# Pre-norm Fourier-attention and gated-MLP layer: wider weight transfers, a fold by column halves, smaller constants, and a new order on five engines

## What is computed

```python
xn = layernorm(x)
q, kv = heads(xn @ W_q.T), heads(xn @ W_kv.T)
qf, kvf = fft(q), fft(kv)                       # along the 32 of a head
qf, kvf = qf / norm(qf), kvf / norm(kvf)        # complex l2 norm of each head
kvf = cumsum(kvf, axis=sequence)
x = x + real(ifft(qf * kvf)) @ W_o.T
h = layernorm(x)
gate = silu((h @ fp8(gate_w)) * gate_scale)
up = (h @ fp8(up_w)) * up_scale
x = x + ((gate * up) @ fp8(down_w)) * down_scale
```

## Time and profile before

| | us |
|---|---|
| time, median of 3 runs | 422.43 (421.98 to 422.79) |
| the profiled execution, its own time | 422.47 |
| its span, first to last instruction | 420.7 |
| TensorE busy | 411.4 (98%) |
| VectorE busy | 281.6 (67%) |
| ScalarE busy | 193.4 (46%) |
| GpSimd busy | 101.9 (24%) |

### The profile page before, as it was taken

The page is one execution under the profiler, slowest core; times in us unless marked ns, Lnnn a source line. Parts: engine busy times, 40 slices in busy tenths (PEclk is TensorE's granted clock), DMA queues, the critical chain, the costliest instruction groups (busy, mean ns, idle before and its releaser), DMA issues.

```text
span 420.7 us, 5465 instructions
## 1 busy us (share of the span) xinstructions
PE 411.4 (98%) x1895; PEld 219.1 (52%) x1895; DVE 281.6 (67%) x496; ACT 193.4 (46%) x322; POOL 101.9 (24%) x107
## 2 busy tenths in 40 slices
PE   8999999899999999999999999999999999999994
PEld 4744454355555554454554564454555555555553
DVE  5998998989999695187685953176774744322234
ACT  3687656576746245436322573255342522132220
POOL 0133641014244222045450031043441001300002
PEclk9999999999999999999999999999999999999999
DMA  8996547600281153241112025320122041200002
GB/s 261 266 247 238 171 106 182 145 2 0 60 240 28 28 74 76 50 151 49 27 27 51 0 50 89 63 81 20 25 27 51 0 89 30 82 2 0 2 0 100
DMA packets 57546, 33.54 MB, mean 80 GB/s; under 512 B 49456, under 2 KB 49840, under 8 KB 57392
## 3 DMA queue, kind: packets, MB, share of 16 engines
q1 hardware_dynamic: 57232, 33.19, 30.9%
q10 hardware_dynamic: 288, 0.02, 0.0%
HBM read 17.44 MB, written 4.19 MB: 51 GB/s over the span
## 4 chain that ended last, share of the span: by engine, by line
PE 79%; SPq 3%; DVE 3%; issue 1%; DMA 1%; POOL 0%; ACT 0%; DVEq 0%
PE bd L447 21%; PE bg L431 20%; PE bu L431 20%; PE ba L348 10%; PE ba L388 7%; SPq L1583 2%; PE ba L361 1%; DMA hT<-ks 1%; SPq L1609 1%; DVE xn L1019 0%; DVE bst L1104 0%; DVE h L1101 0%; DVE zT L1076 0%; SPq L1570 0%; DVE gu L988 0%
## 5 line engine op out<-in xcount | busy, mean ns | idle before, releaser
L447 PE MATMUL bd<-dw,fu 128*128 128x512 f32 x376 | 100.2, 411 | 0.0
L431 PE MATMUL bg<-hT,gu 128*128 128x512 f16 x384 | 91.0, 380 | 1.3 <-DMA hT<-ks 1.3
L431 PE MATMUL bu<-hT,gu 128*128 128x512 f16 x384 | 90.7, 379 | 0.0
L447 PEld LDWEIGHTS bd<-dw,fu 128*128 128x128 f32 x376 | 70.6, 188 | 18.6 <-DVE fu L1146 0.7
L1141 DVE SCALAR_TENSOR_TENSOR ff<-bu,us,sl 128x512 f32<-128x512 f32 x48 | 35.9, 748 | 66.1 <-PE bu L431 62.9
L697 ACT ACTIVATE sl<-bg,gs 128x512 f32<-128x512 f32 x48 | 33.0, 687 | 81.1 <-PE bg L431 80.1
L348 PE MATMUL ba<-wf,xT 128*128 128x512 f16 x288 | 63.2, 379 | 0.0
L431 PEld LDWEIGHTS bu<-hT,gu 128*128 128x128 f16 x384 | 37.6, 98 | 45.3
L431 PEld LDWEIGHTS bg<-hT,gu 128*128 128x128 f16 x384 | 34.9, 98 | 47.8 <-issue 10.2
L1146 DVE TENSOR_TENSOR fu<-ff,fu 128x512 fp32r<-128x512 f32 x47 | 40.0, 852 | 15.7 <-ACT fu L703 15.3
L1504 POOL TENSOR_TENSOR h<-ff,h 128x512 f32<-128x512 f32 x14 | 17.6, 1276 | 129.9 <-DVE ff L1163 129.9
(11 more groups left out here) (174 smaller groups left out, 447.9 us busy)
## 6 DMA issues: line engine op xcount, KB each, us to landing
h<-x_dram SPq DMA_DIRECT2D x16, 256.0 KB, 4.2
out_dram<-h SPq DMA_DIRECT2D x16, 256.0 KB, 2.0
hT<-w_q_dram SPq DMA_DIRECT2D x4, 256.0 KB, 3.7
gu<-w_kv_dram SPq DMA_DIRECT2D x4, 256.0 KB, 4.0
hT<-gate_w_dram SPq DMA_DIRECT2D x2, 512.0 KB, 4.0
hT<-up_w_dram SPq DMA_DIRECT2D x2, 512.0 KB, 6.2
gu<-woT_dram SPq DMA_DIRECT2D x1, 1024.0 KB, 5.2
hT<-down_w_dram SPq DMA_DIRECT2D x2, 512.0 KB, 5.0
```

What stands on the lines that cost most here:

```text
L431: m = e.matmul(bk[:, :], gu[:, c, 4 * w + k, col:col + P], hT[:, b % 2, part, k, :], start=k == 0 and part == 0, stop=k == KT - 1 and part ...
L447: m = e.matmul(bd[t][:, :], fu_at(n)[:, part, P * t:P * t + P], dw[:, i, :], start=i == 0 and part == 0, stop=i == NI - 1 and part == 1)
```

## The change

- W_q and W_kv come in four transfers of two blocks (512 KB) and not in eight of one block; the host lays them out by pairs of blocks. `sum_w` waits for its pair.
- The constant for `pe_heads` is no longer part of `cst`; GpSimd writes it (five memsets, `pool_heads`) into a tile of its own, and `cst` is 128 columns. `dve_head` now waits for `cst`, `pe_heads` for the memsets.
- A bank of the fold holds two slices k and the 256 columns of two blocks, where it held one slice k and all 512 columns. So the first two banks are complete after blocks 0 and 1; `act_wf` and `dve_wf` run on such banks, and `pe_qk` waits for both column halves of a pair of slices.
- `EPS` is a bias in ScalarE's root (from the tile `eps`, a GpSimd memset), and `root0_head` on VectorE is gone. `dve_xl` is gone: `pool_xl` does all tiles.
- One warm-up matmul fewer; `act_first_root` and `dve_one` stand later.
- All five engines have a new order, in the opening, in block 0 and in the loop.

The diff, cut to its core (of the orders, a few lines):

```diff
-        cst = sb("cst", [P, 384], F32)
+        cst = sb("cst", [P, 256], F32)
+        heads = sb("heads", [P, P], F32)
...
+    def folds(w):
+        return [piece for g in range(2) for piece in (("heads", w, g), ("fold", w, g, 0), ("fold", w, g, 1))]
...
         def pe_fold(e, w, f):
-            j = KT * w + f
+            j, g = KT * w + f, f // 2
...
-                if f == 0:
-                    vacant(e, ("fold", w, k))
-                m = e.matmul(ba[AT["fold", w, k]][:, P * f:P * f + P], raw[w][:, f, P * k:P * k + P], fs[:, j, :],
+                if f % 2 == 0 and k % 2 == 0:
+                    vacant(e, ("fold", w, g, k // 2))
+                at = 256 * (k % 2) + P * (f % 2)
+                m = e.matmul(ba[AT["fold", w, g, k // 2]][:, at:at + P], raw[w][:, f, P * k:P * k + P], fs[:, j, :],
...
-                        e.wait_ge(v_wf, 4 * w + k + 1)
+                        e.wait_ge(v_wf, 4 * w + 2 + k // 2 + 1)
...
         def act_root0(e, b, ts):
-            piece = roots_of(b, ts[0])
-            e.wait_ge(v_r1, 2 * piece + 1)
-            e.activation(E1[:, 1, ts[0]:ts[-1] + 1], E1[:, 0, ts[0]:ts[-1] + 1], ACT.Sqrt).then_inc(a_rt0, 1)
+            g = slice(ts[0], ts[-1] + 1)
+            e.wait_ge(p_eps, 1)
+            e.wait_ge(v_mv1, 2 * (4 * b + ts[-1]) + 2)
+            if b > 0:
+                e.wait_ge(v_r1, roots_of(b, 0))
+            e.activation(E1[:, 0, g], mv1[:, g, 1], ACT.Sqrt, bias=eps[:, :]).then_inc(a_rt0, 1)
...
-        def dve_xl(e):
-            e.wait_ge(a_xh, 1)
-            e.tensor_tensor(xs[:, 0, 1, :], xn[:, 0, :], xs[:, 0, 0, :], ALU.subtract).then_inc(v_xl, 1)
...
+        def pool_heads(e):
+            e.memset(heads[:, :], 0.0).then_inc(p_heads, 1)
+            e.wait_ge(p_heads, 1)
+            for q in range(0, P, HD):
+                e.memset(heads[q:q + HD, q:q + HD], 2.0 ** -14).then_inc(p_heads, 1)
...
-        def sp_raw(e, w, f):
-            e.dma_start(raw[w][:, f, :], (w_q, w_kv)[w][P * f:P * f + P, :]).then_inc(d_raw[w][f], 16)
+        def sp_raw(e, w, g):
+            src = (w_q, w_kv)[w][P * g:P * g + P, :]
+            e.dma_start(raw[w][:, 2 * g:2 * g + 2, :], src.rearrange("p (f n) -> p f n", f=2)).then_inc(d_raw[w][g], 16)
```

715 lines of the change are left out of this document (354 added, 361 removed).

## The result

The changed kernel is slower. Median of 5 runs: 426.49 us (425.13 to 427.21), against 422.43 us (421.42 to 422.79) for the kernel before; the ratio is 1.0084, 95% interval 1.0062 to 1.0107. The prediction was 421.1 us with a range up to 423.7. The profiled execution took 426.49 us, its span 424.7 at a granted clock of 0.998.

A forecast was written before the change was run, and what follows sets the result against it. TensorE was taken as the bound, busy 332.55 of 332.70 us, so only its waits could be won. 422.47 - 0.1 (stretch to 45 us) - 1.3 (hT) = 421.1 us, range 419.6 to 423.7.

The forecast's parts named there:

- W_o's state: TensorE's start of the work behind the last high part of W_o: 45.07 us before, forecast at 44.95.
- The opening, steps 1 to 5: Walk to TensorE's second projection: reached at 19.2 us instead of 20.06, 0.8 earlier, range 0.3 to 1.6.
- Step 4: Opening: the transposed input tile 0 lands at 13.6 to 14.4 us, up to 15.4 with full rings.
- step 5: Opening: VectorE's last remainder of folded W_q at about 16.1 us; projection ends at 17.4, two folds make it 19.2.
- Steps 1 to 3: Opening: second pair of W_q at 7.9 us, W_q folded at 12.3, first two folds of W_kv until about 14.3.
- The point on the table load: Opening, ScalarE: a load of 1.28 us between first sum and root, 5.7 to 6.9, is hidden.
- Tile 3: Projection of input tile 3: transposes land at 32.9 us, TensorE arrives at 32.4, a new wait of 0.5 (0 to 1.5).
- W_o: Preparation of W_o: TensorE waits 1.1 us for ScalarE's copy; 0.1 us of the opening's gain is left.
- The wait for hT: Before the first gate matmul: SyncE starts hT's transfers at 66 us, so the whole 1.3 us wait goes.
- The rival "the wait for hT stays": SyncE's queue: the first hT transfer begins at 69 again, the eight take 10 us, time 422.2 us; chance 0.18.
- The rival on VectorE: MLP of block 0: VectorE is late for the first `dve_f`, or the same in the loop, 423.7 us; chance 0.18.
- The rival "opening not shorter": Opening: transposed tile 0 lands at 16 or later, everything to 45 us about 0.8 late, 422.0 to 423; chance 0.11.

The follow-up runs named there:

- the run with the old attention: Changed kernel with block 0's attention, from the second projection to the last dve_hT, in the order of the kernel before: 424.20 us, ratio 1.0037.
- the run with the opening alone: Changed opening, then every engine's remaining work and the loop in the order of the kernel before: 422.53 us, ratio 1.0008 to the kernel before.
- the old loop: Changed kernel with the loop over b = 1 to 3 in the order of the kernel before on all five engines: 426.28 us, ratio 1.0104.

## Why the prediction was wrong, point by point

*What bounds the kernel*: right. TensorE has the same work at the same clock, and the time is what it waits. Against the forecast of 421.1 the changed kernel is 5.4 us longer. W_o's state came 1.9 us later than forecast (46.89, not 44.95), another 2.0 were lost from there to the first gate matmul (84.73, not 80.75: the 1.41 us for hT, and 0.56 us for the transposed z at 57.27, of which the forecast has nothing), and 1.5 behind it, where the forecast took none. No single term explains the direction; the steps that failed follow.

*The opening, steps 1 to 5*: 19.2 forecast, 20.96 in this profile, outside the range of 0.3 to 1.6 us early. Step 4 held: the transposed tile 0 landed at 14.1. In step 5 the last remainder ended at 17.7 and not at 16.1, but the projection, begun at 16.59, did not wait for it. Steps 1 to 3 failed. In this profile the first pair of W_q came late (VectorE's sum at 5.98, 4.54 before), but that is not the reason: in the fourteen other profiles with the same opening that sum begins at 4.69 to 5.53, and TensorE's second projection is still never earlier than 20.00 and up to 21.83. What they share is the order. VectorE's first scalings of `fs` now stand behind the statistics of the second input tile, and wait for its transfer; the clearest case is the run with the old attention:

```profile
7.38 0.69 DVE L1012 BATCH_NORM_STATS2 bst<-h 128x6 f32<-128x512 f32 x1 [1.93 <-DMA h<-x_dram]
...
8.72 0.71 PE L343 MATMUL ba<-fs,hT 128*128 128x128 f32 x4 [1.73 <-DVE fs L984]
```

From the first fold on, all fifteen take 12.7 to 13.7 us to the second projection (12.8 here), where the kernel before takes 12.55 (7.51 to 20.06): the reordering shortens nothing there. Two waits stand in each of them that steps 2 and 3 put at nothing: 0.36 to 0.42 us for the sums of W_kv, ahead of the last fold of W_q (12.47 here), and 0.40 to 0.45 us for the scalings of `fs` beside GpSimd's low part (14.35 here). The move of the low part was counted as 0.6 us taken off VectorE, and it gave 0.9 and 0.5 us back on the two pairs of scalings beside it. The point on the table load held, the load was hidden behind the wait for the second pair:

```profile
6.72 1.28 ACT L620 ACT_TABLE_LOAD   x1
8.02 0.48 ACT L620 ACTIVATE E<-mv,eps 128x1 f32<-128x1 f32 x2
8.40 0.61 ACT L612 ACTIVATE tu<-hT 128x512 f32<-128x512 f32 x1
```

The load begins 0.02 us after the sum's last row has ended (6.70), and the activation behind it starts 0.02 us after its end. The Trainium skill, "ScalarE: Activation LUTs", What ACT_TABLE_LOAD costs, puts a drain of some 1380 ns on top; the trace does not show it here either. And the opening as a whole had the smaller say: the run with the opening alone was 0.5 us late at 20 us and not at all at the end.

*Tile 3*: a wait of 0.5 was forecast and 0.64 came, by luck. The landing time was about right (2.6 to 3.3 us), but ScalarE's high part came at 30.65 and not at 28.1, held by the sums over W_o and a half that waited for their transfers, and TensorE was 2.3 us later than forecast as well (34.67, not 32.4), so that the difference stayed. For tile 2 no wait was forecast, and 0.32 came: the step left out that its transposes stand in a queue into which the same diff puts W_o 5 us earlier, where they took 6.0 to 7.7 us. With the high part of tile 3 early, its transposes met that queue too and took 5.0 to 5.2.

*W_o*: the wait before its fourth part was forecast at 1.1 us and TensorE's state at 44.95. The wait was 0.20 and the state 46.89. The premise "counted from VectorE's clock" was right, but VectorE's clock was not 0 to 1.1 us earlier, it was later: it scaled kv tiles 2 and 3 at 44.16 (42.33). I had set the statistics moved ahead against the work removed and called it even; this is the step that failed. VectorE's first norm alone, behind three more statistics and the late projections, was 3.0 us later than before (33.23, 30.27), and the scaling 1.8.

*The wait for hT*: forecast gone, measured 1.4. Two rows say why:

```profile
70.02 12.26 SPq L1593 DMA_TRANSPOSE hT<-ks  x8
...
77.42 0.69 DVE L1131 TENSOR_TENSOR ks<-qk,ks 128x512 f16<-128x512 f32 x1 [0.53 <-ACT ks L699]
```

The step that failed is the start of SyncE's transfers: 70.02 and not 66. The transposes of an input tile at 65.70, which wait 1.3 us for their high part, and three weight transfers stand ahead of them; I took these to need nothing late. On their way the eight lose another 1.2 us to waits for rows, as the second tile's `dve_hT` ends at 72.77 (68.03 before), and one issue takes 2.4 us in place of 1.25. So the last one is issued at 81.0 and lands 3.4 us later. The last `dve_hT` was wrong as well: it ends at 78.11 and not at 74.7. But it is not what was waited for, since the last pair is issued only 1.65 us after it; with the weights behind hT, SyncE began at 68.23, the last rows were as late (77.91), and there was no wait. The idea itself was right: what decides is when SyncE comes to these transfers, and on the kernel before the same move took the wait away. Its worth was put too high, at the full 1.3 us, where 0.4 us came in the median, not clear of the noise.

*The rival "the wait for hT stays"*: right in its place and its reason, weights and an input tile's transposes ahead of hT (69 assumed, 70.02 measured). Its price was not: by its own figures, a start at 69, eight issues of 1.25 us and a landing of 2.5, the last one lands at 80.3, which makes no wait at all. The waits for rows, the long issue and the longer landing made it one.

*The rival on VectorE*: it alone forecast a slower kernel, but 2.8 us too little of it (423.7), and in the wrong place. The first `dve_f` was not late:

```profile
88.38 0.75 DVE L1145 SCALAR_TENSOR_TENSOR ff<-bu,us,sl 128x512 f32<-128x512 f32 x1 [0.84 <-PE bu L439]
```

The roundings ahead cost instead the norm of block 1, which stood behind them. I followed `dve_f` because TensorE needs it next, and did not follow the work that had been pushed down behind it. The MLP of block 0 took 74.84 us, 1.0 more than before, where the forecast had none.

*The loop*: none forecast; the old loop gave 426.28 against 426.49. Right.

*The rival "opening not shorter"* named what happened at 20 us, but not its reason (it wanted the transposed tile 0 at 16 or later, and it landed at 14.1), and it still took the 1.3 us off for hT; its price of 422 to 423 would have needed that.

What stays open: why each of the two orders costs 1.7 to 2.0 us is followed to late chains (VectorE's norm of block 0; the running sums of block 1) but no run that moved one piece gave time back, so that it is these chains is read from the traces and not shown by removal. That the two orders are the cost, half each, is shown.
